# Graph layer, first of six: the eighth chunk gathered as well, and every edge key decoded before the gathers

## The reference

```python
h = layernorm(x)
for layer in range(6):
    agg = jax.ops.segment_sum(h[src], dst, num_segments=n)
    z = (h + agg) @ W1[layer] + b1[layer]
    z = jax.nn.relu(batchnorm(z, g1[layer], be1[layer]))
    z = z @ W2[layer] + b2[layer]
    z = batchnorm(z, g2[layer], be2[layer])
    h = z if layer == 5 else jax.nn.relu(z)
```

## Time and profile before

| what | us |
|---|---|
| median of three runs | 3790.29 |
| profiled execution, from its first to its last instruction (span; the profile gives no other time of it) | 3784.5 |
| start stage: until the first dense product | 0 to 111.2 |
| first layer: dense steps, windows and slots | 111.2 to 615.5 |
| first layer: batch norm, second product | 615.5 to 655 |
| second layer: its first dense product | 695.9 |

### The profile page before, as it was taken

One profiled execution on the slowest core, in us unless ns is written; L12 is line 12 of the kernel. 1 busy time (PEld: TensorE's weight loads), 2 busy tenths in 40 slices (PEclk: granted clock), 3 DMA queues, 4 the chain that ended last, 5 costly groups with the idle time before them and its releaser, 6 DMA issues.

```text
span 3784.5 us, 69343 instructions
## 1 busy us (share of the span) xinstructions
PE 3634.5 (96%) x26358; PEld 2033.4 (54%) x26358; DVE 2109.3 (56%) x6775; ACT 1416.3 (37%) x2665; POOL 2756.0 (73%) x2845
## 2 busy tenths in 40 slices
PE   2899999999999999999999999999999999999999
PEld 1455554544456555555555555555554555665666
DVE  9988775556465444732227222282223776777766
ACT  6666654200042000510006000060001767677777
POOL 5666664677756777667776677667776799999997
PEclk9999999999999999999999999999999999999999
DMA  6444342668525555255552565535554100000000
GB/s 205 144 127 151 124 151 84 204 220 273 177 100 185 190 173 172 90 186 192 193 182 95 170 207 181 169 128 189 190 177 126 63 22 12 23 12 23 11 16 10
DMA packets 203707, 506.19 MB, mean 134 GB/s; under 512 B 33860, under 2 KB 137872, under 8 KB 196848
## 3 DMA queue, kind: packets, MB, share of 16 engines
q0 software_dynamic: 83360, 227.95, 20.3%
q1 hardware_dynamic: 120016, 273.74, 19.9%
HBM read 412.08 MB, written 89.48 MB: 133 GB/s over the span
## 4 chain that ended last, share of the span: by engine, by line
PE 77%; DVE 9%; ACT 4%; DMA 4%; issue 3%; POOL 3%; SPq 0%; POOLq 0%; ACTq 0%; DVEq 0%
PE bank L1181 47%; PE bank L2428 6%; PE bank L2411 6%; PE bank L2396 5%; PE bank L1217 4%; PE bank L1293 3%; DMA sg<-pieces_d,ssrc 2%; PE bank L983 2%; DVE zh L2167 1%; ACT h L2467 1%; ACT f L2468 1%; DVE st L2192 1%; POOL sg L1518 1%; DVE ohk L782 1%; POOL ry L1406 1%
## 5 line engine op out<-in xcount | busy, mean ns | idle before, releaser
L1181 PE MATMUL bank<-slab,pieces 128*128 128x510 fp8e4 (+1 forms) x9408 | 2321.0, 378 | 5.3 <-DVE slab L801 5.3
L1518 POOL DMA_INDIRECT sg<-pieces_d,ssrc x1322 | 1261.7, 954 | 548.8 <-issue 249.4
L1181 PEld LDWEIGHTS bank<-slab,pieces 128*128 128x128 f16 (+1 forms) x9408 | 800.8, 97 | 668.2 <-DVE slab L801 7.7
L1899 DVE TENSOR_SCALAR so<-iota,skey 128x49 f16<-128x49 f16 (+21 forms) x1322 | 319.1, 262 | 599.5 <-PE bank L1217 598.2
L1423 ACT ACTIVATE z<-bank,prm,ct 128x510 f32<-128x510 f32 (+2 forms) x130 | 94.9, 749 | 1223.2 <-DVE st L1417 1223.2
L1217 PEld LDWEIGHTS bank<-so,sg 128*128 128x128 f16 x5288 | 322.1, 96 | 286.5 <-DMA sg<-pieces_d,ssrc 14.7
L1518 POOL DMA_INDIRECT sgm<-pieces_d,ssrc x400 | 380.7, 952 | 121.8 <-issue 90.8
L2686 POOL TENSOR_SCALAR btmp<-bob,rw 128x256 f32<-128x256 f32 (+1 forms) x343 | 400.3, 1167 | 33.5
L2467 ACT ACTIVATE h<-bank,fscale 128x512 f16<-128x512 f32 (+2 forms) x416 | 314.8, 757 | 186.4 <-PE bank L2411 186.1
L1217 PE MATMUL bank<-so,sg 128*128 128x51 f16 (+20 forms) x5288 | 343.2, 182 | 9.3 <-DMA sg<-pieces_d,ssrc 9.2
L930 ACT ACTIVATE slab<-bank 128x490 fp8e4<-128x490 f32 x408 | 278.4, 695 | 141.3 <-PE bank L983 138.1
(11 more groups left out here) (355 smaller groups left out, 3946.0 us busy)
## 6 DMA issues: line engine op xcount, KB each, us to landing
slab<-slabs SPq DMA_DIRECT2D x40, 3123.8 KB
pieces_d<-pieces SPq DMA_DIRECT2D x60, 512.0 KB
slabs<-slab SPq DMA_DIRECT2D x8, 3123.8 KB, 11.9
sg<-pieces_d,ssrc POOLq DMA_INDIRECT x1322
mx<-xnorm SPq DMA_DIRECT2D x24, 512.0 KB
ws<-L_ffn_W_dram SPq DMA_DIRECT2D x32, 256.0 KB, 8.1
sgm<-pieces_d,ssrc POOLq DMA_INDIRECT x400
experts<-wp SPq DMA_DIRECT2D x24, 256.0 KB, 4.1
```

Source lines behind the costliest of these rows:

```text
L1181: ins = pe.matmul(psD[half][:, 0:w], PC[:k, a, c:c + P], v[:k, a, :], start=(r == 0), stop=(r == 97))
L1518: pool.indirect_dma_start(out=SG[j % ring_of(l)][:, :], out_offset=None, in_=d_H[:, :], in_offset=bass.IndirectOffsetOnAxis(ap=SI[:, j:j + ...
L1899: dve.tensor_scalar(SO[j % ring_of(l)][:, 0:w], iota[:, 0:w], SK[:, j:j + 1], None, ALU.is_equal).then_inc(s_soh, 1)
```

## The change

In the first layer chunk 7 is gathered as well, after the chunks 8 to 12 (`GATHERED`), and its 196 dense steps are left out there. Its slab is still built and stored for the other five layers. The slots of the first layer now lie from step 44 to step 1336 of 1372; windows stand every 1.85 steps, in the seventh chunk every 1.6. Four rows of slot keys are loaded and decoded in place of three. VectorE splits the bits of all rows 1 to 6 right behind the first keys, in six buffers of their own instead of two; GpSimd decodes all of them directly behind the slot keys; rows 4 and 5 are transposed in the start stage, row 6 at step 6. The first gather is placed at step 4 instead of step 72. The check sums the first seven slabs twice, and every slot but those of chunk 7 twice, so that the total is 2E. Some small buffers have other places.

```diff
+ND0 = NDC - 1
+GATHERED = list(range(NDC, NCH)) + [NDC - 1]
+NGC = len(GATHERED)
+NSB = 4
...
 def plan_slots():
     slots = []
-    for t in range(NDC, NCH):
+    for t in GATHERED:
...
+def nslot(l):
+    return NSLOT0 if l == 0 else NSLOT
+def slots_before(l):
+    return NSLOT0 + NSLOT * (l - 1) if l else 0
+def ndense(l):
+    return NDC if l else ND0
+def slab_used(n):
+    return 2 * min(n + 1, ND0) if n < NDC else 2 * n
...
     if l == 0:
-        for t in range(NDC - 1):
+        for t in range(ND0):
             for i in range(CWIN):
-                add(STEPS * t + 1.9 * i, "window", CWIN * (t + 1) + i)
-        add(0, "bits", 4)
-        add(2, "bits", 5)
-        add(38, "keys", 4)
-        add(40, "bits", 6)
-        add(72, "keys", 5)
-        add(106, "keys", 6)
-        add(STEPS * (NDC - 1) + 60, "flag_sum")
-        add(STEPS * (NDC - 1) + 130, "flag_end")
-        g0, g1 = 112, STEPS * NDC - 100
+                add(STEPS * t + (1.6 if t == ND0 - 1 else 1.85) * i, "window", CWIN * (t + 1) + i)
+        add(6, "keys", 6)
+        add(STEPS * (ND0 - 1) + 166, "flag_sum")
+        add(STEPS * (ND0 - 1) + 184, "flag_end")
+        g0, g1 = 44, STEPS * ND0 - 36
...
-    for t in range(NDC):
+    for t in range(ndense(l)):
         for s in range(STEPS):
...
-    out.append(("zin", NDC - 1, 1))
-    out.extend(("gemm1", NDC - 1, q) for q in (0, 2, 1, 3))
+    out.append(("zin", ND0 - 1, 1))
+    out.extend(("gemm1", ND0 - 1, q) for q in (0, 2, 1, 3))
+    out.append(("slab_next", NDC - 1))
...
     def dve_key_bits(w):
         dve.wait_ge(s_row[w], 16)
-        if w > 2:
-            dve.wait_ge(s_kk, w + 1)
-        dve.tensor_scalar(phl[w % 2][:, 0, :], GE_T[w][:, 256:512], 7, None, ALU.logical_shift_right)
+        dve.tensor_scalar(phl[w - 1][:, 0, :], GE_T[w][:, 256:512], 7, None, ALU.logical_shift_right)
...
         dve_first_keys()
+        for w in range(1, DTILES):
+            dve_key_bits(w)
         windows = iter(range(CWIN + 8))
         for u in range(1, 8):
...
-            if 3 <= u <= 5:
-                dve_key_bits(u - 2)
...
+            act.wait_ge(s_kk, NSB + DTILES - 1)
...
             if u <= 3:
                 pe_turn_slots(u - 1)
-            if 4 <= u <= 6:
+            if u == 3:
+                pe_turn_slots(3)
+            if u >= 4:
                 pe_turn_keys(u - 3)
         for w in range(7 * LINKS, CWIN + 8):
             pe_window(w - 8)
+        pe_turn_keys(5)
...
     def pool_start():
-        for w in (0, 7, 8, 9, 1, 2, 3, 4, 5, 6):
+        for w in (0, 7, 8, 9, 10, 1, 2, 3, 4, 5, 6):
...
         pool_slot_keys(0)
-        for u in range(1, 8):
-            if u < 3:
-                pool_slot_keys(u)
-            if 3 <= u <= 5:
-                pool_keys(u - 2)
+        for w in range(1, NSB):
+            pool_slot_keys(w)
+        for w in range(1, DTILES):
+            pool_keys(w)
...
-                    sp.wait_ge(s_dense, 2 * (n - 2) + 2)
+                    sp.wait_ge(s_dense, slab_used(n - 2))
                     sp.dma_start(slab_view(n % NDC, n), d_A[n % NDC, :, :]).then_inc(s_slab[n % 2], 16)
```

More of the change, by code:

```diff
@@ L72, with gathered, dense_before, first_slot @@
 SLOTS = plan_slots()
-NSLOT = len(SLOTS)
 LAST_SLOT = {t: i for i, (t, s, lo, w) in enumerate(SLOTS)}
-SROWS = (NSLOT + 2) // 3
+NSLOT = LAST_SLOT[NCH - 1] + 1
+NSLOT0 = len(SLOTS)
+SROWS = (NSLOT0 + NSB - 1) // NSB
+def gathered(l):
+    return GATHERED if l == 0 else GATHERED[:-1]
+def nslot(l):
[4 more added lines that the diff above has]
+    return NDC if l else ND0
+def dense_before(l):
+    return 2 * ND0 + 2 * NDC * (l - 1) if l else 0
+def slab_used(n):
+    return 2 * min(n + 1, ND0) if n < NDC else 2 * n
+def first_slot(t):
+    p = GATHERED.index(t)
+    return LAST_SLOT[GATHERED[p - 1]] + 1 if p else 0
 CMPW = DTILES * P
@@ L204, in side_work @@
     add(max(0, g0 - 40), "fetch_first")
[L205 to L208, removed]
+    per = (g1 - g0) / nslot(l)
+    for i, (t, s, lo, w) in enumerate(SLOTS[:nslot(l)]):
+        i0, n = first_slot(t), LAST_SLOT[t] + 1
+        begin, end = g0 + per * i0 + (BETWEEN if i0 else 0), g0 + per * n
         g = begin + (end - begin) * (s + 1) / (n - i0)
@@ L483, in build @@
     SL = [at(f"slab{i}", [P, NT * CH], F8, R_SL + 24992 * i) for i in range(2)]
-    ZIN = [at(f"zin{i}", [P, 2, 2, (CH, WIDTHS[-1])[i]], F16, R_ZIN + 4096 * i) for i in range(2)]
+    ZIN = [at(f"zin{i}", [P, 2, 2, CH], F16, R_ZIN + 4096 * i) for i in range(2)]
     ZH = at("zh", [P, 2, 2 * N], F16, R_Z)
@@ L609, in build @@
     ms = [part(f"ms{i}", [P, 32], F32) for i in range(5)]
-    mxt = [part("mxt0", [P, 2, P], F32), at("mxt1", [P, 2, P], F32, R_KEEP + 6176)]
+    mxt = [at(f"mxt{i}", [P, 2, P], F32, o) for i, o in enumerate((R_ZIN + 1216 * MORE, R_KEEP + 6176))]
     free["at"] = R_F
@@ L720, in keys_at @@
     def keys_at(w):
-        return 1 if w == 0 else w + 4
+        return 1 if w == 0 else w + 1 + NSB
     def win_bank(pr):
@@ L1134, in fetch_count @@
         r = i % ring_of(l)
-        uses = sum(len(range(r, NSLOT, ring_of(k))) for k in range(l) if r < ring_of(k))
-        return (1 if r < RINGS else 0) + uses + i // ring_of(l) + 1
+        uses = sum(len(range(r, nslot(k), ring_of(k))) for k in range(l) if r < ring_of(k))
+        return (1 if r < DTILES + NSB else 0) + uses + i // ring_of(l) + 1
     def gram_rows(g):
@@ L1221, in pe_layer @@
                 m, k = item[2] // 2, item[2] % 2
-                w, b = width(i), 0 if i < NDC else 1
+                w, b = width(i), 1 if i in gathered(l) else 0
                 if item[2] == 0:
@@ L2743, in constants @@
 def constants():
-    cf = np.zeros((P, 2 * P + DTILES + 10 + 3 * NSC), np.float32)
-    last = 2 * P + DTILES + 9
-    cf[0:8, last] = cf[16:24, last] = 1.0
+    first = 2 * P + DTILES
+    cf = np.zeros((P, first + 4 * NSB + NSB * NGC), np.float32)
     cf[:, 0:P] = np.eye(P)
@@ L2752, in constants @@
         j, r = divmod(i, SROWS)
-        o = 2 * P + DTILES + 3 * j
-        cf[r, o:o + 3] = (FIRST_NODE[t] + lo, w, P // FINE * s)
-        cf[r, last + 1 + NSC * j + t - NDC] = 1.0
+        cf[r, first + 3 * j:first + 3 * j + 3] = (FIRST_NODE[t] + lo, w, P // FINE * s)
+        cf[r, first + 3 * NSB + j] = 2.0 if t >= NDC else 1.0
+        cf[r, first + 4 * NSB + NGC * j + GATHERED.index(t)] = 1.0
     return {
```

160 lines of the change are left out of this document (84 added, 76 removed).

## The result

The kernel after takes 3801.65 us (median of 19 runs, 3795.39 to 3806.9), the kernel before beside it 3792.07 (19 runs, 3788.36 to 3795.49): ratio 1.0024, 95% interval [1.0017, 1.003]. It is slower by 9.6 us, where 16 us less were forecast. The spans of the two profiled executions are 3784.5 and 3799.8 us, 15.3 apart. In every run on record that lists both, the span is 3.7 to 4.2 us shorter than the time. By that, an estimate, the profiled execution before took some 3788.4 us, 3.7 under its median, and the one after, 3803.65 us, lies 2.0 over its own: the traces show about 6 us more than the medians.

A forecast was written before the change was run, and what follows sets the result against it. GpSimd's gathers were to bound the first layer, with TensorE close: first gather 134 + 448 + issue, landing and tail = 596.5 us against 613.9, 17.4 less, 1.4 given back; 3790.3 - 16 = 3774.3 us, range 3759 to 3788.

The forecast's parts named there:

- GpSimd's total: First layer, first gather to last: 354 intervals of 1.255 us plus one stretched issue of 3.7, 448 us.
- the stores of the slabs: Rival: seven 3.1 MB stores stretch gathers beyond the ring's 12.5 us, costing 23 us, time 3797; chance 0.07.
- TensorE's total: First layer's aggregation: products, chunk boundaries and low clock at the start together 454 us, against 504.5 before.
- The first dense product: End of the start stage: moves from 111.2 to about 122 us, bounds 114 to 131.
- The bit splits and loads: Start stage: VectorE's six bit splits wait for the last edge load before the first window, +4.8 us (+2.3 to +7.4).
- The decodings: Start stage: GpSimd decodes three more key rows there, slowing VectorE's one-hots, +6 us (0 to +12).
- The first gather: First chunk: waits for the pieces' last store, 12 us after the first dense product (9 to 15), at 134.
- The base of the forecast: Whole kernel: median 3790.3 us, 5.8 above the profiled span of 3784.5, taken as time around the span.
- the 1.4 already given: First layer: 1.4 us given back from the 17.4 us gain for TensorE's low clock after waits.
- The dearer start: Rival, start stage: decodings stretch the tail by 4.5 us and the load lands late, 3783 to 3792; chance 0.14.
- VectorE starving the gathers: Rival, first layer: one gather issue in ten stretched by 3.7 us, 130 us in all, near 3904; chance 0.02.
- GpSimd idle on the ring: Sign against the forecast: it is wrong if GpSimd waits for free gather buffers in the first layer; no size given.

The follow-up runs named there:

- e7: The kernel before with each first-layer slab stored in seven spread parts, nothing else changed: 3789.21 us, ratio 0.9991 to the kernel before.
- e5: The kernel after with slab stores in seven parts, bit splits at the units' ends and 96-row slot edge loads together: 3777.13 us, ratio 0.9962 to before.
- e4: The kernel after with key rows 5 and 6 split and decoded in the first chunk, after the start stage: 3806.97 us, ratio 1.0038 to before.
- e10: The kernel before with only the start stage's part of the change, chunk 7 still dense: 3792.39 us, ratio 1.0001 to before.
- e11: Chunk 7 gathered as in the kernel after, but with the start stage of the kernel before: 3796.33 us, ratio 1.0008 to before.
- e8: The kernel after with each slab stored a second time, to a tensor nobody reads: 3828.61 us, ratio 1.0097 to before.
- e1: The kernel after with each first-layer slab stored in seven parts, one every 14 windows of the next chunk: 3784.05 us, ratio 0.998 to before.
- e6: The kernel after with seven-part stores, bit splits in the units, 96-row loads and the last pieces stored earlier: 3767.69 us, ratio 0.9939 to before.

## Why the prediction was wrong

*The step that failed* is the one that made GpSimd's total 354 x 1.255 + 3.7 = 448 us and set the stores of the slabs aside as a rival of 7 in 100. From the first gather to the last it measured 466.4 us; with the stores spread, 451.4. The intervals were right, the stores were not in the sum. My argument against them was that TensorE never waits for a gather beside a store in the kernel before, and that the ring of ten covers 12.5 us of landing. The observation was right (e7: their cost there is about nothing). It doesn't carry over, because a ring covers only what is in it. In chunks two to seven before, 249 slots in 381 us are one per 1.53 us, and GpSimd can issue one per 1.25: it runs ahead until the ring is full, which is why most of its idle time ended with a slot's product; ten slots are then 15 us of cover. Afterwards TensorE wants a slot about every 1.25 us on the average, as the prediction itself worked out, and GpSimd gives one in 1.25. That average hides a rhythm: inside a chunk TensorE takes a slot every 1.05 us (18 of them from 251.35 to 270.19), behind a chunk's end it has weight products as well and takes slots more slowly, and there GpSimd catches up. The store of a slab is issued just where the chunk ends, when the ring is emptiest. Counted in the timelines, the gather nearest to each of the first six stores beside gathers was issued 14.4 to 21.5 us ahead of its slot before, with seven to nine others in the ring. Afterwards two to five others were in the ring:

```profile
251.35 0.26 PE L1254 MATMUL bank<-so,sg 128*128 128x41 f16 x4
...
270.19 0.26 PE L1254 MATMUL bank<-so,sg 128*128 128x52 f16 x4
```

At 273 us the gather is 5.3 us ahead of its use. A landing of 10 to 12 us, inside the 12.5 that I had granted, then stops TensorE for 6 to 7 us. Towards the end of the layer the lead is larger, 7.1 us at 488.04, and the same landing costs 3.3. While TensorE stands, GpSimd fills the ring and stops in turn: ten gathers go from 273.61 to 284.92, and the next waits 2.09 us, until 287.95. So the time is lost for both.

*TensorE's total* of 454 us was not measured by itself, but fits. The stage took 497.5: 454, and 35.7 of waits for gathers in place of some 20, and a rest of 7.8, low clock for the most part, of which I had given 1.4. The granted clock falls to 0.50 in the wait, the 1.2 GHz level, and is back at 0.89 in the next 4 us. I took the stage as the longer of two paths, GpSimd's 12 + 448 + 14.5 = 474.5 and TensorE's 454. Where both are that close, a delay on either side can add to both; this is argued from the rhythm above and not measured by itself.

*The first dense product* was to come at 122 (114 to 131), and came at 127.7, inside the bounds. The bit splits and loads were +4.8 in my sum (+2.3 to +7.4) and measured 8.2 (after against e5). The row counts of the slot keys, whose fourth row I had at 0 to 1, are behind the difference: a row now covers 89 slots in place of 96, and four loads of 2.03 us stand where three of 0.91 stood, so the last load is issued at 32.15 and not at 27.4. Also it is the first of the six rows, not the last, that VectorE waits for; the other five had landed by then or within 0.15 us. The decodings were +6 and measured 2.5 a row (e4), 7.6 for three: the one-hots `ohk` of the tail take 366 ns on the average where they took 280. Together 15.8 of the 16.5.

*The first gather* came 15.0 us after the first dense product, at the far bound, in place of 12: the pieces' last store is issued at 133.3 to 136.8, 5.6 to 9.1 behind as forecast, and landed 6 us later.

*The base of the forecast* was off by a little as well. I put the 5.8 us between the median and the span down to what lies around the span. Of these some 3.9 belong there, and the rest is that the profiled execution was a fast one.

*The sum of these:* 5.7 (first dense) + 3.0 (first gather) + 18.4 (gathers) + 1.6 (from the last gather to the end) = 28.7 on the 596.5 of the forecast, or 625.2, where the last dense product ends. Less the 1.4 already given, that is 27.3 on the -16, and gives the 11.3 of the trace.

*The rivals.* The stores are the one that came, with 3797 forecast and 3801.65 measured, but by another condition than its own: it was to begin where a landing exceeds 12.5 us. That the two times lie so close is in part luck: it had 23 us for the stores, which cost 17.6, and nothing for the dearer start. The dearer start was right in sign and came on top of it. VectorE starving the gathers didn't happen: the longest issue is 1.57 us, the median 0.946. The sign that I had named, GpSimd idle on the ring, came too: 118 times, 53.9 us in all, of which some 35 are the pause of 0.30 that each gather has. Neither part of the change alone is a gain: the start alone changes nothing (e10, 0.0 us to the kernel before beside it), and the gathering alone is 4 us slower, with an interval that contains no change (e11).

*What stays open.* The packets show the gathers all but held beside a store, and not why. The Trainium skill ("DMA: Bandwidth & Descriptors", Queues, rings and completion order) says that each DMA engine takes turns between its queues, a packet at a time. By it a gather would be slowed beside a large store and not held until its end. The trace agrees in part: from 279 to 281 us the gathers' queue moves about one packet for each of the store's, but from 276 to 279 one for 48.

```profile
q1 hardware_dynamic: 48, 1.20, 93.4%
q0 software_dynamic: 1, 0.00, 0.0%
```

Why the second store of e8 cost no more than it did is open as well, and whether it is the smaller packets or the spreading that helps in e1. A full ring, by contrast, is seen to be enough: in the kernel before, with the same whole stores, TensorE waits for none of the gathers beside the first six.

## What to carry to other kernels

Before work moves to an engine with room, divide the time of the stage by the number of its items: when the two sides of a ring come close to one rate, the ring no longer runs full, and delays that it hid before show. Count, in the timeline, how many items are in the ring when the longest landing begins. Then look at what large transfers stand beside the small ones, and cut them into parts that are spread over the stage (17.6 and 19 us here, for the same bytes in smaller packets). And ask what the first item of the new bottleneck waits for: moving that (e6) was worth 9.4 us, while a shorter stage in front of it was worth nothing (e4).

## What the runs showed of the hardware

The time that an indirect load occupies GpSimd depends on the number of its rows in a way that I had not expected. 89 rows take 2.03 us and 97 take 2.16, where 90, 96, 100, 112 and 128 take 0.97, 0.92, 0.98, 1.05 and 0.95 (97, 90, 100 and 112 rows were seen once each). Only the two primes are dear. The Trainium skill ("DMA: Bandwidth & Descriptors", Why a DMA increments its semaphore by 16 and not by 1) says that a transfer is split over the largest number of DMA engines up to 16 that divides its rows; by this rule 89 and 97 rows go to one engine, 90 to fifteen, 100 to ten, and the measured times agree with it in kind. The number of engines itself was not read from a trace. A row count that falls out of a division, as 355 / 4 does here, is best rounded up.

Beside a whole slab store the DMA engines moved 415 GB/s, the gathers' share fell from 1.04 MB in 10 us to 0.06 MB in 4 us, and a gather of 128 rows issued with the store landed in 10.0 to 12.2 us. With the slab stored in sevenths, the gathers of the chain landed in at most 5.5 us.
